# Splitting the kept weights on GpSimd and dividing the mix on ScalarE in a fused attention and feed-forward kernel

## The chip, the cores and the metric

One core of a Trainium2 chip runs the whole kernel. The metric is the device time of one execution in microseconds (us). The engines are TensorE (PE in the profile), its weight loader (PEld), VectorE (DVE), ScalarE (ACT), GpSimd (POOL) and SyncE (SP), which issues the DMAs of weights and output.

## The reference

Eight blocks (the batch) of 128 rows and 512 columns pass through a layer norm, a cross-attention with 32 query heads in 8 groups, a residual add, and a feed-forward stage that looks up a mix of 64 bias rows:

```python
x = x + _L0_xattn_ref(_layernorm(x, axis=-1), ctx_4096, ctx_4096, pos_BxS2, mask_BxSxS2_ik0, Wq, Wk, Wv, Wo)
x = x + _L0_ffn_ref(_layernorm(x, axis=-1), router_weight, router_bias, expert_bias)

def _L0_ffn_ref(hidden_states, router_weight, router_bias, expert_bias):
    logits = jnp.einsum('th,eh->te', flat, router_weight) + router_bias      # 64 logits a row
    scores = jax.nn.softmax(logits, axis=-1)
    topk_w, topk_idx = jax.lax.top_k(scores, K_TOP)                          # K_TOP = 8
    w_sum = topk_w.sum(axis=-1, keepdims=True)
    w_dense = jnp.zeros((T, E), dtype=scores.dtype).at[jnp.arange(T)[:, None], topk_idx].add(topk_w)
    bias_mix = jnp.einsum('te,eh->th', w_dense, expert_bias)
    out = flat * w_sum + bias_mix
```

So a row's output is x + layernorm(x) * w_sum + the mix of the eight kept rows of expert_bias.

## The kernel before

Every engine has its own program, written in the order in which it runs; the engines wait for one another by semaphores that count up. Attention runs over 8 groups (g) and in each over the 8 blocks (b), one block a **step**. In a step TensorE computes the scores of the block two ahead, transposes the probabilities (probT), multiplies block b-1 by Wo into outp, multiplies probabilities and values into attnT, and projects a query seven steps ahead. Numbers are split into a high and a low part (names with _hi and _lo) for the matmuls; ScalarE makes the high part and VectorE or GpSimd the low one.

The feed-forward stage is woven into the 8 steps of the last group (g = 7, `last=True`) and a tail behind them. "Step 4" is below always step 4 of the last group. The stage of a block b is spread over steps:

- step b+1: `ffn_stats(b)` on VectorE (ff_stats, ff_mv, ff_var), then `ffn_rstd(b)` on GpSimd (ff_rstd, ff_mr).
- step b+2: TensorE transposes the block and forms its 64 logits in bank proj[0]; VectorE closes the step with `ffn_max(b)`: ff_shift, ff_logit, ff_negmax. ScalarE, which waits for ff_negmax, then makes ff_exp, and behind it in its order v_hi and pT_hi of the next step.
- step b+3: `ffn_keep(b)` on VectorE: the eight largest (ff_top), ff_rest (the exponentials with those eight set to zero), ff_rsum = 1/sum, ff_kept = ff_exp - ff_rest, and ff_kept split into ff_split. TensorE transposes ff_split (`ffn_kept`, L1185, just before the last head's Wo matmuls of the step), ScalarE copies it to ff_splitT, TensorE multiplies it by the split expert_bias (`ffn_mix`, L1193 and L1194) into bank proj[1], GpSimd makes ff_weight, ff_scale and ff_bias, ScalarE ff_y = x * scale + bias, and VectorE closes the block in `ffn_out`: ff_out = mix * ff_rsum + ff_y. SyncE stores ff_out.

The order on VectorE in step b of the last group is mask_scores, `ffn_keep(b-3)`, lo_p (pT_lo), row_max (negmax), accumulate (resid), `ffn_stats(b-1)`, invert_sums, lo_o (oT_lo), `ffn_max(b-2)`, `ffn_out(b-3)`. Steps 6 and 7 have no scores left, so no mask_scores, row_max or softmax division (GpSimd's `soften`, L412). On ScalarE the order is v_hi, pT_hi, ff_splitT, ff_xT, ff_y, the four exponentials (probs), oT_hi, ff_exp. TensorE's instructions are in one row too: where the transposition of ff_split waits, the Wo matmuls, the probability times value matmuls and the logits stand behind it. Blocks 5 to 7 of the feed-forward stage end in the tail.

Of the kernel before, what the change touches and what calls it, by code (L numbers as in the profile page):

```python
# [19 lines left out]
F32 = mybir.dt.float32  # L20
# [3 lines left out]
ALU = mybir.AluOpType  # L24
ACT = mybir.ActivationFunctionType
# [3 lines left out]
B, S, E = 8, 128, 512  # L29
# [38 lines left out]
FF = 2  # L68
# [3 lines left out]
def xattn_ffn(nc, x, ctx, pos, mask, rope, wq, wk, wv, wo, router, router_bias, expert_bias, out):  # L72
    with ExitStack() as stack:
# [3 lines left out]
        def at(name, cols, dt, offset, parts=P):  # L77
            return nc.alloc_sbuf_tensor_at(name, [parts] + cols, dt, offset=base + int(offset * kib))
# [4 lines left out]
        def sem(name):  # L83
            return stack.enter_context(nc.semaphore(name))
# [15 lines left out]
        ff_y = at("ff_y", [FF, E], F32, 58)  # L100
# [3 lines left out]
        ff_out = at("ff_out", [2, E], F32, 68)  # L104
        ff_logit = at("ff_logit", [NX], F32, 72)
        ff_exp = at("ff_exp", [FF, NX], F32, 72.25)
        ff_rest = at("ff_rest", [FF, NX], F32, 72.75)
        ff_kept = at("ff_kept", [NX], F32, 73.25)
# [53 lines left out]
        ff_top = at("ff_top", [TOP], F32, 206.65625)  # L162
        ff_kept_sum = at("ff_kept_sum", [1], F32, 206.6875)
        ff_rsum = at("ff_rsum", [FF], F32, 75.25)
        ff_weight = at("ff_weight", [1], F32, 75.28125)
        ff_scale = at("ff_scale", [2], F32, 75.3125)
        ff_bias = at("ff_bias", [2], F32, 75.34375)
# [88 lines left out]
        f_rsum = sem("f_rsum")  # L256
# [10 lines left out]
        f_keptT = sem("f_keptT")  # L267
        f_keptTs = sem("f_keptTs")
        f_mix = sem("f_mix")
        f_out = sem("f_out")  # L270

        def projection_bank(u):
# [90 lines left out]
        def _(pool):  # L363
# [46 lines left out]
            def soften(p, count):  # L410
                pool.wait_ge(rsum_done, count)
                pool.tensor_tensor(probs[:, p], probs[:, p], rsum[:, p, :].unsqueeze(2).broadcast_to([P, GH, S]),  # L412
                                   ALU.mult).then_inc(soft_done, 1)
# [18 lines left out]
            def step(g, b, first=False, last=False):  # L432
                n = b + g * B
                if not (first and b < 2):
                    lo_v(g, b, first)
                if not (first and b == 0) and not (last and b + AHEAD - 1 >= B):
                    rotate((KV * NH + AHEAD - 1 + b, g, B), (b + AHEAD - 1) // GH % NH)
                if b < GH and not last:
                    lo_a(wq_lo[:, b], wq_hi[:, b], b % RA, A_Q + GH + b + 1 + g * GH)
                if b == 0 and not first:  # L440
                    for h in range(GH):
                        lo_b(wo_lo[:, h, :], wo_hi[:, h, :], h, KB * C + h + 1 + g * GH)
                if last and b == 0:
                    pool.wait_ge(f_ebhi, 1)
                    pool.tensor_tensor(ff_eb_lo[:, :], ebias[:, :], ff_eb_hi[:, :].bitcast(F32), ALU.subtract).then_inc(f_eblo, 1)
                if last:
                    ffn(b)
                if first and b == 0:
                    lo_v(0, 1, True)
                if not (last and b + FIRST >= B):  # L450
                    soften(b % 2, n + FIRST + 1)

            def ffn(b):
                if b >= 3:
                    ffn_weight(b - 3)
                if 1 <= b < B + 1:
                    ffn_rstd(b - 1)

            def ffn_rstd(b):

                pool.wait_ge(f_var, b + 1)
                if b >= 2:
                    pool.wait_ge(f_bias, b - 1)
                pool.tensor_tensor(ff_rstd[:, b % 2:b % 2 + 1], ff_var[:, :], power[:, 0:1], ALU.pow).then_inc(f_rstd, 1)
                pool.wait_ge(f_rstd, b + 1)
                pool.tensor_tensor(ff_mr[:, b % 2:b % 2 + 1], ff_mv[:, 0:1], ff_rstd[:, b % 2:b % 2 + 1], ALU.mult).then_inc(f_mr, 1)

            def ffn_weight(b):

# [19 lines left out]
                    step(g, b)  # L489
            for b in range(B):  # L490
                step(KV - 1, b, last=True)
            for b in range(B, B + 3):
                ffn(b)


# [1 line left out]
        def _(act):  # L497
# [146 lines left out]
            def ffn(b, part):  # L644
                if part == 0 and b >= 3:
                    ffn_kept(b - 3)
                if part == 0 and b >= 2:
                    ffn_xT(b - 2)
                if part == 0 and b >= 3:
                    ffn_scale(b - 3)  # L650
                if part == 1 and b >= 2:
                    ffn_exp(b - 2)

            def ffn_xT(b):
                act.wait_ge(f_xT, b + 1)
                if b >= 1:
                    act.wait_ge(f_raw, b)
                act.activation(ff_xT[:, :], logit_bank[b][:, :], ACT.Copy).then_inc(f_xTs, 1)

            def ffn_scale(b):  # L660

                act.wait_ge(f_scale, b + 1)
                act.wait_ge(f_bias, b + 1)
                if b >= FF:
                    act.wait_ge(f_out, b - FF + 1)
                act.activation(ff_y[:, b % FF, :], resid[:, b, :], ACT.Identity,
                               bias=ff_bias[:, b % 2:b % 2 + 1], scale=ff_scale[:, b % 2:b % 2 + 1]).then_inc(f_y, 1)

            def ffn_exp(b):
                act.wait_ge(f_max, b + 1)  # L670
# [20 lines left out]
            ffn_kept(B - 3)  # L691
            ffn_exp(B - 2)
            ffn_scale(B - 3)
            ffn_xT(B - 1)
            ffn_kept(B - 2)
            ffn_exp(B - 1)
# [6 lines left out]
        def _(dve):  # L703
# [183 lines left out]
            def ffn(b, part):  # L887
                if part == 0 and b >= 3:
                    ffn_keep(b - 3)
                if part == 1 and b >= 1:  # L890
                    ffn_stats(b - 1)
                if part == 2 and b >= 2:
                    ffn_max(b - 2)
                if part == 2 and b >= 3:
                    ffn_out(b - 3)

            def ffn_stats(b):

# [29 lines left out]
            def ffn_keep(b):  # L928

                exp, rest = ff_exp[:, b % FF, :], ff_rest[:, b % FF, :]  # L930
                dve.wait_ge(f_exp, b + 1)
                dve.max(ff_top[:, :], exp).then_inc(f_top, 1)
                dve.wait_ge(f_top, b + 1)

                dve.match_replace(rest, ff_top[:, :], exp, 0.0).then_inc(f_rest, 1)
                if b >= 2:
                    dve.wait_ge(f_out, b - 1)
                dve.reciprocal(ff_rsum[:, b % FF:b % FF + 1], ff_sum[:, b % FF:b % FF + 1]).then_inc(f_rsum, 1)
                dve.wait_ge(f_rest, b + 1)
                dve.tensor_tensor(ff_kept[:, :], exp, rest, ALU.subtract).then_inc(f_kept, 1)  # L940
                if b >= 1:
                    dve.wait_ge(f_weight, b)
                dve.tensor_reduce(ff_kept_sum[:, :], ff_top[:, :], X_AXIS, ALU.add).then_inc(f_ksum, 1)
                dve.wait_ge(f_kept, b + 1)
                if b >= 1:
                    dve.wait_ge(f_keptT, b)
                dve.tensor_copy(ff_split[:, 0, :], ff_kept[:, :]).then_inc(f_khi, 1)
                dve.wait_ge(f_khi, b + 1)
                dve.tensor_tensor(ff_split[:, 1, :], ff_kept[:, :], ff_split[:, 0, :].bitcast(F32), ALU.subtract).then_inc(f_klo, 1)

            def ffn_out(b):

                dve.wait_ge(f_y, b + 1)
                if b >= 2:
                    dve.wait_ge(dma_out[b % 2], 16 * (b // 2))
                dve.wait_ge(f_mix, b + 1)
                dve.scalar_tensor_tensor(ff_out[:, b % 2, :], mixes[b][:, :], ff_rsum[:, b % FF:b % FF + 1], ff_y[:, b % FF, :],
                                         ALU.mult, ALU.add).then_inc(f_out, 1)
# [11 lines left out]
            ffn_stats(B - 1)  # L970
            ffn_keep(B - 2)
            ffn_max(B - 1)
            ffn_out(B - 3)
            ffn_keep(B - 1)
            ffn_out(B - 2)
            ffn_out(B - 1)
# [3 lines left out]
        def _(pe):  # L980
# [152 lines left out]
            def ffn(b, part):  # L1133
                if part == 0 and b >= 2:
                    ffn_xT(b - 2)
                if part == 0 and b >= 3:
                    ffn_kept(b - 3)
                if part == 1 and b >= 2:
                    ffn_logits(b - 2)
                if part == 1 and b >= 3:  # L1140
                    ffn_mix(b - 3)
# [32 lines left out]
            def ffn_kept(b):  # L1174

                pe.wait_ge(f_klo, b + 1)
                if b == 0:
                    pe.wait_ge(f_colsums, 1)
                elif b < B - 2:
                    pe.wait_ge(f_out, b)  # L1180
                elif b == B - 2:
                    pe.wait_ge(exp_done, STEPS)
                else:
                    pe.wait_ge(ot_lo, STEPS)
                pe.transpose(mixes[b][:, 0:S], ff_split[:, :, :].rearrange("p a k -> p (a k)").bitcast(F32), ident[:, :]).then_inc(f_keptT, 1)  # L1185
# [79 lines left out]
```

## Time and profile before

| | us |
|---|---|
| median of 3 runs (lowest to highest) | 622.12 (621.84 to 622.55) |
| the profiled execution, own time | 622.68 |
| its span in the trace | 620.8 |
| TensorE busy, of the span | 603.8 |
| VectorE busy | 421.0 |
| ScalarE busy | 347.2 |
| GpSimd busy | 323.1 |

The profiled execution lies 0.56 us above the median; the span is shorter than its own time by 1.9 us of start and end. TensorE is busy for almost the whole span, but the stage around the change is the last 50 us, and whether TensorE waits there is read from that stretch alone.

### The profile page before, as it was taken

The numbers are of one execution on the slowest core, as the hardware profiler recorded it, in microseconds if no ns is written. First come the engines' busy times: TensorE is split into PE (matmuls) and PEld (weight loads), VectorE is DVE, ScalarE is ACT, GpSimd is POOL, SyncE is SP. The second block draws the span as 40 slices with busy tenths as digits, with TensorE's granted clock in tenths as the row PEclk, the third lists the DMA queues.
The fourth block names the chain that finished last, engine by engine and source line by source line (L and its number), as shares of the span: only waits on it lengthen the run. The fifth ranks groups of instructions, "written<-read, shape, count | busy, mean of one in ns | idle before, by whom it ended". The sixth has DMA issues, their size and how long they took to land.

```text
span 620.8 us, 10479 instructions
## 1 busy us (share of the span) xinstructions
PE 603.8 (97%) x3076; PEld 505.9 (81%) x3076; DVE 421.0 (68%) x730; ACT 347.2 (56%) x1008; POOL 323.1 (52%) x342
## 2 busy tenths in 40 slices
PE   8999999899999999999999999999999999999986
PEld 7787888688888888888888888888888888888774
DVE  5565667677667766776677667666766776667886
ACT  5222556476557556655665565557555755575553
POOL 5340778665338533853484347435743664374331
PEclk9999999899999999999999999999999999999997
DMA  8710132201003100310021003000300120000001
GB/s 293 276 59 11 35 119 51 69 21 50 0 1 103 34 1 1 101 34 0 0 101 34 0 0 117 18 0 11 108 17 0 32 70 0 0 2 2 34 35 68
DMA packets 16025, 29.58 MB, mean 48 GB/s; under 512 B 2048, under 2 KB 2176, under 8 KB 16000
## 3 DMA queue, kind: packets, MB, share of 16 engines
q1 hardware_dynamic: 15472, 28.22, 14.6%
q0 software_dynamic: 384, 1.05, 0.5%
q8 instruction: 12, 0.20, 0.1%
q14 instruction: 13, 0.11, 0.1%
q10 hardware_dynamic: 144, 0.00, 0.0%
HBM read 27.17 MB, written 2.10 MB: 47 GB/s over the span
## 4 chain that ended last, share of the span: by engine, by line
PE 85%; POOL 4%; DVE 4%; issue 2%; ACT 2%; DMA 1%; SPq 0%; DVEq 0%; POOLq 0%; ACTq 0%
PE proj L983 11%; PE proj L985 10%; PE proj L984 10%; PE outp L1129 9%; PE outp L1131 9%; PE outp L1130 8%; PE score L1084 8%; PE probT L1097 4%; PE attnT L983 2%; PE outp L985 2%; PE outp L983 2%; PE attnT L985 2%; PE outp L984 2%; PE attnT L984 2%; POOL rot L368 2%
## 5 line engine op out<-in xcount | busy, mean ns | idle before, releaser
L574 ACT ACTIVATE probs<-score,negmax 128x128 f32<-128x128 f32 x256 | 90.3, 366 | 61.2 <-DVE negmax L811 61.2
L368 POOL TENSOR_TENSOR rot<-rot,sinT 128x512 f32<-128x512 f32 x80 | 106.9, 1336 | 30.6 <-ACT rot L506 30.6
L505 ACT ACTIVATE rot<-proj 64x512 f32<-64x512 f32 x72 | 42.7, 594 | 126.7 <-PE proj L985 126.7
L803 DVE SCALAR_TENSOR_TENSOR score<-score,mask_bias 128x512 f32<-128x512 f32 x64 | 44.7, 698 | 97.3 <-PE score L1084 97.3
L412 POOL TENSOR_TENSOR probs<-probs,rsum 128x512 f32<-128x512 f32 x64 | 66.6, 1040 | 83.1 <-DVE rsum L817 83.1
L1129 PE MATMUL outp<-wo_hi,oT_hi 128*128 128x512 f32 x256 | 107.2, 419 | 2.6 <-DVE oT_lo L846 2.3
L983 PE MATMUL proj<-xT_hi,wq_hi 128*128 128x512 f32 x256 | 100.9, 394 | 0.0
L1131 PE MATMUL outp<-wo_hi,oT_lo 128*128 128x512 f32 x256 | 100.7, 394 | 0.0
L985 PE MATMUL proj<-xT_hi,wq_lo 128*128 128x512 f32 x256 | 100.2, 391 | 0.0
L984 PE MATMUL proj<-xT_lo,wq_hi 128*128 128x512 f32 x256 | 100.1, 391 | 0.0
L1130 PE MATMUL outp<-wo_lo,oT_hi 128*128 128x512 f32 x256 | 100.0, 391 | 0.0
L712 DVE TENSOR_TENSOR qT<-qT,rot 128x512 f32<-128x512 f32 x64 | 76.9, 1202 | 27.8 <-POOL rot L368 27.7
L420 POOL TENSOR_TENSOR v_lo<-values,v_hi 128x128 fp32r<-128x128 f32 x64 | 29.5, 462 | 124.9 <-ACT v_hi L581 124.9
L1084 PEld LDWEIGHTS score<-kT,qT 128*128 128x128 f32 x512 | 66.8, 191 | 8.2 <-issue 2.7
L1084 PE MATMUL score<-kT,qT 128*128 (+1 forms) x512 | 67.9, 276 | 2.5 <-DVE qT L712 2.3
L1129 PEld LDWEIGHTS outp<-wo_hi,oT_hi 128*128 128x128 f32 x256 | 48.4, 189 | 12.2 <-DVE oT_lo L846 4.5
L1131 PEld LDWEIGHTS outp<-wo_hi,oT_lo 128*128 128x128 f32 x256 | 48.0, 188 | 11.4
L983 PEld LDWEIGHTS proj<-xT_hi,wq_hi 128*128 128x128 f32 x256 | 48.5, 189 | 10.7 <-issue 0.6
L985 PEld LDWEIGHTS proj<-xT_hi,wq_lo 128*128 128x128 f32 x256 | 48.3, 189 | 10.3
L984 PEld LDWEIGHTS proj<-xT_lo,wq_hi 128*128 128x128 f32 x256 | 48.5, 189 | 9.9
L1130 PEld LDWEIGHTS outp<-wo_lo,oT_hi 128*128 128x128 f32 x256 | 48.4, 189 | 8.2
L574 ACT ACTIVATION_READ_ACCUMULATOR probs<-score,negmax 128x1 f32 x256 | 52.1, 204 | 0.0
(181 smaller groups left out, 1146.6 us busy)
## 6 DMA issues: line engine op xcount, KB each, us to landing
ring_a<-in_wq SPq DMA_DIRECT2D x32, 256.0 KB, 2.6
ring_b<-in_wo SPq DMA_DIRECT2D x32, 256.0 KB, 2.5
ctx_in<-in_ctx SPq DMA_DIRECT2D x8, 256.0 KB, 4.2
ring_b<-in_wv SPq DMA_DIRECT2D x8, 256.0 KB, 7.6
resid<-in_x SPq DMA_DIRECT2D x2, 1024.0 KB, 12.0
ring_a<-in_wk SPq DMA_DIRECT2D x8, 256.0 KB, 2.6
out<-ff_out SPq DMA_DIRECT2D x8, 256.0 KB, 2.0
mask_in<-in_mask SPq DMA_DIRECT2D x1, 512.0 KB, 11.9
```

The source lines that it names most:

```text
L368: pool.tensor_tensor(rot[:, k0 % 2, :], rot[:, k0 % 2, :], sinT[:, half * W:(half + 1) * W], ALU.mult).then_inc(sin_done, 1)
L412: pool.tensor_tensor(probs[:, p], probs[:, p], rsum[:, p, :].unsqueeze(2).broadcast_to([P, GH, S]), ALU.mult).then_inc(soft_done, 1)
L574: last = act.activation(probs[:, p, h, :], heads(score[p][:, :])[:, h, :], ACT.Exp, bias=negmax[:, p, h:h + 1], accum_out=sums[:, p, h:h + 1])
L712: dve.tensor_tensor(dst, dst, rot[:, k % 2, :], ALU.add).then_inc(rope_done, 1)
L803: dve.scalar_tensor_tensor(heads(score[p][:, :]), heads(score[p][:, :]), SCALE, mask_bias[:, b, :].unsqueeze(1).broadcast_to([P, GH, S]), ...
L983: pe.matmul(ps, s_hi, m_hi, start=start, stop=False)
L984: pe.matmul(ps, s_hi, m_lo, start=False, stop=False)
L985: return pe.matmul(ps, s_lo, m_hi, start=False, stop=stop)
L1084: last = pe.matmul(score[p][:, h * S:(h + 1) * S], qT[:, half % 2, h, b % HB * S:(b % HB + 1) * S], kT[:, b0 // B + g, b * S:(b + 1) * S], ...
L1129: pe.matmul(outp[b % 2][:, :], oT_hi[:, cols], w[0], start=h == 0, stop=False)
L1130: pe.matmul(outp[b % 2][:, :], oT_hi[:, cols], w[1], start=False, stop=False)
L1131: pe.matmul(outp[b % 2][:, :], oT_lo[:, cols], w[0], start=False, stop=h == GH - 1).then_inc(o_done, 1)
```

## The change

For the first six blocks three pieces move. The subtraction that gives ff_kept and its split into two halves go from VectorE's `ffn_keep` to a new `ffn_keep` on GpSimd, ahead of `ffn_weight`. VectorE's fused multiply and add becomes two operations: ScalarE copies the mix out of PSUM scaled by ff_rsum (new tile ff_mix, new semaphore f_mixed, new `ffn_mixed`, behind oT_hi and ahead of ff_exp), and GpSimd adds ff_mix and ff_y (new `ffn_out`, behind `soften`). The last two blocks keep their operations on VectorE. TensorE's transposition of ff_split now waits for f_mixed of the block before, where it waited for f_out; SyncE's code is unchanged, its stores wait for f_out as before.

```diff
@@ gpsimd
                 if not (last and b + FIRST >= B):
                     soften(b % 2, n + FIRST + 1)
+                if last and b >= 3:
+                    ffn_out(b - 3)

             def ffn(b):
+                if 3 <= b < B + 1:
+                    ffn_keep(b - 3)
                 if b >= 3:
                     ffn_weight(b - 3)
...
+            def ffn_keep(b):
+
+                pool.wait_ge(f_rest, b + 1)
+                if b >= 1:
+                    pool.wait_ge(f_klo, b)
+                pool.tensor_tensor(ff_kept[:, :], ff_exp[:, b % FF, :], ff_rest[:, b % FF, :], ALU.subtract).then_inc(f_kept, 1)
+                pool.wait_ge(f_kept, b + 1)
+                if b >= 1:
+                    pool.wait_ge(f_keptT, b)
+                pool.tensor_copy(ff_split[:, 0, :], ff_kept[:, :]).then_inc(f_khi, 1)
+                pool.wait_ge(f_khi, b + 1)
+                pool.tensor_tensor(ff_split[:, 1, :], ff_kept[:, :], ff_split[:, 0, :].bitcast(F32), ALU.subtract).then_inc(f_klo, 1)
+
+            def ffn_out(b):
+
+                pool.wait_ge(f_mixed, b + 1)
+                pool.wait_ge(f_y, b + 1)
+                if b >= 2:
+                    pool.wait_ge(dma_out[b % 2], 16 * (b // 2))
+                pool.tensor_tensor(ff_out[:, b % 2, :], ff_mix[:, b % FF, :], ff_y[:, b % FF, :], ALU.add).then_inc(f_out, 1)
...
-            for b in range(B, B + 3):
+            ffn(B)
+            ffn_out(B - 3)
+            for b in range(B + 1, B + 3):
                 ffn(b)
@@ scalar
+                if part == 1 and b >= 3:
+                    ffn_mixed(b - 3)
                 if part == 1 and b >= 2:
                     ffn_exp(b - 2)
...
+            def ffn_mixed(b):
+
+                act.wait_ge(f_mix, b + 1)
+                act.wait_ge(f_rsum, b + 1)
+                if b >= FF:
+                    act.wait_ge(f_out, b - FF + 1)
+                act.activation(ff_mix[:, b % FF, :], mixes[b][:, :], ACT.Copy, scale=ff_rsum[:, b % FF:b % FF + 1]).then_inc(f_mixed, 1)
...
             ffn_scale(B - 3)
+            ffn_mixed(B - 3)
             ffn_xT(B - 1)
@@ vector
-                if part == 2 and b >= 3:
-                    ffn_out(b - 3)
...
-                dve.wait_ge(f_rest, b + 1)
-                dve.tensor_tensor(ff_kept[:, :], exp, rest, ALU.subtract).then_inc(f_kept, 1)
                 if b >= 1:
                     dve.wait_ge(f_weight, b)
                 dve.tensor_reduce(ff_kept_sum[:, :], ff_top[:, :], X_AXIS, ALU.add).then_inc(f_ksum, 1)
+                if b < B - 2:
+                    return
+                dve.wait_ge(f_rest, b + 1)
+                dve.wait_ge(f_klo, b)
+                dve.tensor_tensor(ff_kept[:, :], exp, rest, ALU.subtract).then_inc(f_kept, 1)
...
             ffn_max(B - 1)
-            ffn_out(B - 3)
             ffn_keep(B - 1)
@@ tensor
                 elif b < B - 2:
-                    pe.wait_ge(f_out, b)
+                    pe.wait_ge(f_mixed, b)
```

The first place is VectorE in step 4, from the ff_negmax that closes the step before to pT_lo. Before:

```order
L926 TENSOR_REDUCE ff_negmax<-ff_logit 128x1
L957 SCALAR_TENSOR_TENSOR ff_out<-proj,ff_rsum,ff_y 128x512
L803 SCALAR_TENSOR_TENSOR score<-score,mask_bias 128x512
L932 MAX ff_top<-ff_exp 128x8
L935 MATCH_REPLACE ff_rest<-ff_top,ff_exp 128x64
L938 RECIPROCAL ff_rsum<-ff_sum 128x1
L940 TENSOR_TENSOR ff_kept<-ff_exp,ff_rest 128x64
L943 TENSOR_REDUCE ff_kept_sum<-ff_top 128x1
L947 CAST ff_split<-ff_kept 128x64
L949 TENSOR_TENSOR ff_split<-ff_kept,ff_split 128x64
L840 TENSOR_TENSOR pT_lo<-probT,pT_hi 128x512
```

And now:

```order
L964 TENSOR_REDUCE ff_negmax<-ff_logit 128x1
L843 SCALAR_TENSOR_TENSOR score<-score,mask_bias 128x512
L970 MAX ff_top<-ff_exp 128x8
L975 MATCH_REPLACE ff_rest<-ff_top,ff_exp 128x64
L978 RECIPROCAL ff_rsum<-ff_sum 128x1
L981 TENSOR_REDUCE ff_kept_sum<-ff_top 128x1
L880 TENSOR_TENSOR pT_lo<-probT,pT_hi 128x512
```

Four instructions have left VectorE: ff_out between ff_negmax and the mask, and the three that end in ff_split.

The second place is GpSimd in step 4 (block 1 of the feed-forward stage), from the low part of the values to the last instruction of the step. Before:

```order
L420 TENSOR_TENSOR v_lo<-values,v_hi 128x128
L474 TENSOR_TENSOR ff_weight<-ff_kept_sum,ff_rsum 128x1
L480 TENSOR_SCALAR ff_scale<-ff_weight,ff_rstd 128x1
L482 TENSOR_SCALAR ff_bias<-ff_weight,ff_mr 128x1
L464 TENSOR_TENSOR ff_rstd<-ff_var,power 128x1
L466 TENSOR_TENSOR ff_mr<-ff_mv,ff_rstd 128x1
L412 TENSOR_TENSOR probs<-probs,rsum 128x512
```

And now:

```order
L422 TENSOR_TENSOR v_lo<-values,v_hi 128x128
L479 TENSOR_TENSOR ff_kept<-ff_exp,ff_rest 128x64
L483 CAST ff_split<-ff_kept 128x64
L485 TENSOR_TENSOR ff_split<-ff_kept,ff_split 128x64
L501 TENSOR_TENSOR ff_weight<-ff_kept_sum,ff_rsum 128x1
L507 TENSOR_SCALAR ff_scale<-ff_weight,ff_rstd 128x1
L509 TENSOR_SCALAR ff_bias<-ff_weight,ff_mr 128x1
L470 TENSOR_TENSOR ff_rstd<-ff_var,power 128x1
L472 TENSOR_TENSOR ff_mr<-ff_mv,ff_rstd 128x1
L414 TENSOR_TENSOR probs<-probs,rsum 128x512
L493 TENSOR_TENSOR ff_out<-ff_mix,ff_y 128x512
```

The three small instructions stand behind v_lo and ahead of ff_weight; the add is last, behind the softmax division.

The third place is GpSimd in the tail, from the rstd of block 7. Before:

```order
L464 TENSOR_TENSOR ff_rstd<-ff_var,power 128x1
L466 TENSOR_TENSOR ff_mr<-ff_mv,ff_rstd 128x1
L474 TENSOR_TENSOR ff_weight<-ff_kept_sum,ff_rsum 128x1
L480 TENSOR_SCALAR ff_scale<-ff_weight,ff_rstd 128x1
L482 TENSOR_SCALAR ff_bias<-ff_weight,ff_mr 128x1
```

And now:

```order
L470 TENSOR_TENSOR ff_rstd<-ff_var,power 128x1
L472 TENSOR_TENSOR ff_mr<-ff_mv,ff_rstd 128x1
L493 TENSOR_TENSOR ff_out<-ff_mix,ff_y 128x512
L501 TENSOR_TENSOR ff_weight<-ff_kept_sum,ff_rsum 128x1
L507 TENSOR_SCALAR ff_scale<-ff_weight,ff_rstd 128x1
L509 TENSOR_SCALAR ff_bias<-ff_weight,ff_mr 128x1
```

The add of block 5 now stands between ff_mr of block 7 and the weights of block 6.

## Rows read from the trace of the kernel before

**Rows 1.** The page: busy time of each engine, and the chain that ended last.

```profile
PE 603.8 (97%) x3076; PEld 505.9 (81%) x3076; DVE 421.0 (68%) x730; ACT 347.2 (56%) x1008; POOL 323.1 (52%) x342
PE 85%; POOL 4%; DVE 4%; issue 2%; ACT 2%; DMA 1%; SPq 0%; DVEq 0%; POOLq 0%; ACTq 0%
```

**Rows 2.** Timeline, VectorE, steps 3 to 6: start, us, what, idle before.

```profile
569.92 0.22 DVE L926 TENSOR_REDUCE ff_negmax<-ff_logit 128x1 f32<-128x64 f32 x1
...
571.00 0.21 DVE L935 MATCH_REPLACE8 ff_rest<-ff_top,ff_exp 128x64 f32<-128x64 f32 x1
...
577.22 0.22 DVE L926 TENSOR_REDUCE ff_negmax<-ff_logit 128x1 f32<-128x64 f32 x1
577.36 0.74 DVE L957 SCALAR_TENSOR_TENSOR ff_out<-proj,ff_rsum,ff_y 128x512 f32<-128x512 f32 x1
578.02 0.69 DVE L803 SCALAR_TENSOR_TENSOR score<-score,mask_bias 128x512 f32<-128x512 f32 x1
578.62 0.21 DVE L932 MAX8 ff_top<-ff_exp 128x8 f32<-128x64 f32 x1
...
579.68 0.22 DVE L949 TENSOR_TENSOR ff_split<-ff_kept,ff_split 128x64 fp32r<-128x64 f32 x1
...
584.31 0.51 DVE L916 SCALAR_TENSOR_TENSOR ff_shift<-ff_colsum,ff_mr,rbias 128x64 f32<-128x64 f32 x1
...
585.17 0.22 DVE L926 TENSOR_REDUCE ff_negmax<-ff_logit 128x1 f32<-128x64 f32 x1
...
593.12 0.22 DVE L926 TENSOR_REDUCE ff_negmax<-ff_logit 128x1 f32<-128x64 f32 x1
...
599.32 0.22 DVE L926 TENSOR_REDUCE ff_negmax<-ff_logit 128x1 f32<-128x64 f32 x1
```

**Rows 3.** Timeline, TensorE: the transposition of ff_split, and one mix.

```profile
572.07 0.27 PE L1185 MATMUL proj<-ident,ff_split 128*128 128x128 f32 x1
...
579.96 0.33 PE L1185 MATMUL proj<-ident,ff_split 128*128 128x128 f32 x1 [0.67 <-DVE ff_split L949]
...
595.26 0.33 PE L1185 MATMUL proj<-ident,ff_split 128*128 128x128 f32 x1
...
597.95 0.40 PE L1194 MATMUL proj<-ff_eb_lo,ff_splitT 128*128 128x512 f32 x1
```

**Rows 4.** Timeline, GpSimd, steps 3 and 4.

```profile
570.90 0.46 POOL L420 TENSOR_TENSOR v_lo<-values,v_hi 128x128 fp32r<-128x128 f32 x1 [0.29 <-ACT v_hi L581]
...
583.70 1.04 POOL L412 TENSOR_TENSOR probs<-probs,rsum 128x512 f32<-128x512 f32 x1
```

**Rows 5.** Timeline, ScalarE, end of steps 3 and 4.

```profile
577.48 0.35 ACT L674 ACTIVATE ff_exp<-ff_logit,ff_negmax 128x64 f32<-128x64 f32 x1 [1.75 <-DVE ff_negmax L926]
...
583.05 0.62 ACT L635 ACTIVATE oT_hi<-attnT 128x512 fp32r<-128x512 f32 x1
```

**Rows 6.** Timeline, GpSimd, first group: instructions back to back.

```profile
106.45 1.30 POOL L377 TENSOR_TENSOR wo_lo<-ring_b,wo_hi 128x512 fp32r<-128x512 f32 x1
107.71 1.73 POOL L368 TENSOR_TENSOR rot<-rot,sinT 128x512 f32<-128x512 f32 x1
```

**Rows 7.** Timeline, VectorE, the same place.

```profile
106.53 1.77 DVE L712 TENSOR_TENSOR qT<-qT,rot 128x512 f32<-128x512 f32 x1 [0.59 <-POOL rot L368]
```

**Rows 8.** Timeline, GpSimd, the tail.

```profile
612.03 0.19 POOL L466 TENSOR_TENSOR ff_mr<-ff_mv,ff_rstd 128x1 f32<-128x1 f32 x1
612.19 0.19 POOL L474 TENSOR_TENSOR ff_weight<-ff_kept_sum,ff_rsum 128x1 f32<-128x1 f32 x1
612.48 0.30 POOL L480 TENSOR_SCALAR ff_scale<-ff_weight,ff_rstd 128x1 f32<-128x1 f32 x1
```

**Rows 9.** Timeline, VectorE, the tail.

```profile
612.31 0.23 DVE L949 TENSOR_TENSOR ff_split<-ff_kept,ff_split 128x64 fp32r<-128x64 f32 x1
...
612.90 0.28 DVE L923 SCALAR_TENSOR_TENSOR ff_logit<-probT,ff_rstd,ff_shift 128x64 f32<-128x64 f32 x1 [0.17 <-DVE ff_shift L916]
...
614.01 0.22 DVE L932 MAX8 ff_top<-ff_exp 128x8 f32<-128x64 f32 x1
```

More of the change, by code:

```diff
@@ L164, in xattn_ffn @@
         ff_rsum = at("ff_rsum", [FF], F32, 75.25)
+        ff_mix = at("ff_mix", [FF, E], F32, 76)
         ff_weight = at("ff_weight", [1], F32, 75.28125)
@@ L269, in xattn_ffn @@
         f_mix = sem("f_mix")
+        f_mixed = sem("f_mixed")
         f_out = sem("f_out")
@@ L933, in ffn_keep @@
                 dve.wait_ge(f_top, b + 1)
+                if b >= 2:
+                    dve.wait_ge(f_kept, b - 1)
                 dve.match_replace(rest, ff_top[:, :], exp, 0.0).then_inc(f_rest, 1)
@@ L953, in ffn_out @@
                 dve.wait_ge(f_y, b + 1)
-                if b >= 2:
-                    dve.wait_ge(dma_out[b % 2], 16 * (b // 2))
+                dve.wait_ge(f_out, b)
+                dve.wait_ge(dma_out[b % 2], 16 * (b // 2))
                 dve.wait_ge(f_mix, b + 1)
```

## The prediction

> **What bounds the kernel now.** I read the page first, then the timeline of the last 50 us engine by engine. TensorE is busy for 97% of the span and holds 85% of the chain that ended last [rows 1], but those are averages, and the change touches only steps 3 to 7 of the last group and the tail. There I measure each step between two starts of ff_negmax, called N: 569.92, 577.22, 585.17, 593.12, 599.32 [rows 2]. So step 3 lasts 7.30, steps 4 and 5 7.95 each, step 6 6.20, and step 7 repeats step 6. In step 4 TensorE stands idle 0.67 before it transposes ff_split, waiting for VectorE [rows 3], so the step is a loop: ff_negmax, ff_out, mask, ff_top to ff_split on VectorE; then from TensorE's transposition at 579.96 over ScalarE's copies, y and exponentials and VectorE's oT_lo and ff_shift to the next N at 585.17, which is 5.21 [rows 2, 3]. In step 6 that second part is 599.32 - 595.26 = 4.06 (no scores, it runs over the Wo matmuls and the residual add). VectorE's freed time therefore counts only where it makes the transposition start earlier. Everything turns on one figure: how long after N TensorE can transpose ff_split. Now it is 2.15 in step 3 (572.07), 2.74 in steps 4 and 5 (579.96), 2.14 in step 6 (595.26).
>
> **The steps, part by part.** *ff_out leaves VectorE*: its slot is 578.02 - 577.36 = 0.66 [rows 2]. But ff_top needs ff_exp, which ScalarE starts 0.26 after N. Step 3 has no ff_out yet and shows what is left then: ff_rest starts at 571.00, N + 1.08, and ends at N + 1.29. With ff_out, ff_top started at N + 1.40 in step 4 [rows 2]. In steps 6 and 7 there is no mask, ff_out only fills the wait for ff_exp, and its leaving is worth nothing.
>
> *The split on GpSimd*: it needs ff_rest (N + 1.29) and stands behind v_lo, which starts at N + 0.98 (570.90) and lasts 0.46 [rows 4]; instructions there overlap by 0.04 (106.45 + 1.30 against 107.71) [rows 6]. So it starts at N + 1.40. No row shows these three on GpSimd. v_lo, 128 elements, is 0.46, ff_weight, one element, 0.19 [rows 4, 8]; a line through both gives 0.32 for 64 elements with two inputs, and I take 0.26 for the one-input cast. Dependent instructions lie 0.10 apart (ff_weight ends 612.38, ff_scale starts 612.48) [rows 8]. The chain is x = 0.32 + 0.10 + 0.26 + 0.10 + 0.32 = 1.10. TensorE followed ff_split's end by 0.06 (579.68 + 0.22 against 579.96) [rows 2, 3]. The transposition now starts at N + 1.40 + x + 0.06 = N + 2.56. Bounds of x: 0.75 if each takes ff_weight's 0.19 (with 0.18 of gaps), 1.56 if each takes v_lo's 0.46. The value between is nearest in size to both.
>
> The Trainium skill, GPSIMD Engine Reference, section 4.1 Engine selection, speaks against this move: it puts elementwise adds and subtractions on VectorE, GpSimd being about twice as slow with two inputs. Doubling 0.22, 0.20 and 0.22 makes x about 1.46, an estimate from that page, and a total near 626.0.
>
> Against the present steps this gives
> - step 3: 2.56 + 5.21 = 7.77, +0.47
> - steps 4 and 5: 7.77 against 7.95, -0.18 each
> - step 6: 2.56 against 2.14, +0.42
> - step 7: the same +0.42, and 0.1 more: the mix of block 3 ends 3.09 behind the transposition (598.35 against 595.26) [rows 3], ScalarE's scaled copy takes 0.7 (oT_hi is 0.62 [rows 5], a scale pointer more), GpSimd's add 1.30, which ends at about N + 1.1 and holds v_lo up.
>
> Sum: +1.05; as a function of x, 5x - 4.46.
>
> *Costs taken as nothing.* ff_mixed on ScalarE: in steps 3 to 5 it starts at oT_hi's end (583.67), ends near 584.4, and ff_exp waits for ff_negmax until 0.26 after N with 1.75 idle [rows 5]; in steps 6 and 7 half a microsecond of the cover is left. Without it the 0.7 would fall on ff_exp and on each step. The add on GpSimd in steps 3 to 5 follows the division, which ends 584.74 = N - 0.43 [rows 4], ends near N + 0.95, just ahead of v_lo at N + 0.98: hidden with nothing to spare. ff_weight, ff_scale, ff_bias move behind the split: bias ends near N + 3.3, ff_y can't start before the transposition + 1.02 = N + 3.58. TensorE's wait on f_mixed is met a step early; the stores of SyncE end a step ahead of use.
>
> **A lock between VectorE and GpSimd.** ff_shift, two SBUF inputs of 64 elements, takes 0.51 in step 4 (its logit twin, with one input in PSUM, 0.28 [rows 9]); it ends at 584.82, 0.08 after GpSimd's division of the probabilities ends at 584.74 [rows 2, 4]. qT <- qT,rot likewise took 1.77, held until 0.55 after wo_lo's end. It was then served ahead of GpSimd's next instruction, which stretched to 1.73 [rows 6, 7]. So in steps 3 to 5 ff_shift should again get through between the division and the add. ff_rest, with one tensor input, kept 0.21 under v_lo [rows 2, 4]; I let the other one-input instructions pass freely.
>
> In the tail it costs. GpSimd's order is now ff_mr of block 7, the add of block 5, then the weights [rows 8]. The add's inputs are there, so it starts at 612.19, when VectorE has the split of block 6 (612.31) and ff_shift of block 7 still to do [rows 9], both with two SBUF inputs. The add lasts 1.30, to 613.49; the split ends 0.08 later, 613.57; from its end to ff_logit it was 0.36 (612.54 to 612.90) [rows 9], so ff_logit starts at 613.93, +1.03. ff_out of block 5 leaves VectorE there, worth 0.05 at most (ff_top at 614.01 then waits for ff_exp); the cast of blocks 6 and 7 directly follows ff_kept, 0.1 more. Tail: +1.08. All behind it shifts along: the last transposition, mix and store. The tail up to the last Wo matmuls is TensorE's own and takes the split of block 5 with some 0.5 to spare. The tail's bounds are +0.1 (VectorE gets in first) and +1.4.
>
> The Trainium skill, SBUF — State Buffer, section SBUF: two separate sides, calls this an exclusive lock held for a whole instruction by whichever started first. By it the add would hold both VectorE instructions out until it ends; this trace agrees, with the 0.51 above. Who goes first when both wait it doesn't say.
>
> **Sum.** +1.05 + 1.08 = +2.13. On the profiled execution's own 622.68 that is 624.8; the median of the runs is 0.56 lower, so I predict 624.3.
>
> **The rivals.**
> - *No stall in the tail* (12%): the add of block 5 starts after 612.7 instead of 612.2, so VectorE's two instructions go first. Then +1.05 + 0.1: 623.3. Against it: GpSimd followed ff_mr with the next instruction after 0.16 [rows 8].
> - *Short instructions* (6%): x = 0.75. Steps -0.7, tail +1.08: 622.5.
> - *Long instructions* (8%): x = 1.56, as v_lo: steps +3.34, tail +1.08: 626.5.
> - *The lock goes the other way* (6%): the add follows the division before the waiting ff_shift, 1.3 more in each of steps 3 to 5: 628.2. Rows 6 and 7 speak against it.
> - *Faster* (6%): VectorE is the pacer of steps 4 and 5 and is relieved of 1.17 in each. If x were 0.48 (three of 0.10 and the small gaps) the transposition would come at N + 1.94, each of the two steps 0.80 shorter; step 3 and 6 gain nothing, because TensorE gets there at N + 2.15 by itself. With no stall in the tail: -1.5, 620.6. It decides at x below 0.63 and no stall; GpSimd's shortest here, 0.19 for one element, is against it.
>
> **How the numbers follow.** The forecast has 62%, its own range is 623.4 to 625.2. Low 622.6 to high 626.6 takes in the first and third rival and leaves out 18%. A measurement of this kernel tells 0.2% (1.24 us, 623.36) from no change: slower holds 0.62 + 0.08 + 0.06 = 0.76, within it 0.12 + 0.06 = 0.18, faster 0.06.
>
> **What would show it.** In the profile after: the transposition of ff_split at N + 2.5 to 2.6 in every step with GpSimd as releaser, instead of 2.15, 2.74 and 2.14; steps of about 7.8 where they were 7.30 and 7.95, and 6.6 where they were 6.2; GpSimd's three small ones at 0.32, 0.26, 0.32; ff_mix 0.7 with ff_exp still waiting behind; in the tail a split or ff_shift on VectorE stretched to more than 1 us, ending 0.1 behind GpSimd's add. Wrong it would be if x is far from 1.10 (five steps count it), if ff_shift in steps 3 to 5 is longer than 0.5, or if the tail's add lies elsewhere.

## The result and the profile after

Over 20 executions each, the changed kernel takes 623.07 us (622.01 to 626.60) and the kernel before 621.89 (620.55 to 623.32). The ratio is 1.0028 with a 95% interval of 1.0016 to 1.0040: slower by 1.7 us, between 1.0 and 2.5. The ratio is that of the means, 623.38 and 621.64; the medians differ by 1.18. The prediction was slower, by 2.1, with a median of 624.3.

The two profiled executions have the same span, 620.8, although the kernels differ. One profiled execution lost some 1.5 us, and the other did not, in a stretch that the change does not touch. The next rows are windows of the kernel before, 109 to 125 us: length, busy time and count of PE, PEld, DVE, ACT, POOL, then the granted clock, DMA share, GB/s.

```profile
109.00:118.00 9.00, 6.73 (x32) 5.13 (x31) 7.07 (x6) 4.82 (x8) 9.00 (x7) 1.00 0.36 95
118.00:125.00 7.00, 7.00 (x31) 5.87 (x30) 2.86 (x5) 2.69 (x10) 2.23 (x3) 0.76 0.10 27
```

The same windows of the changed kernel:

```profile
109.00:118.00 9.00, 6.75 (x31) 5.07 (x31) 7.07 (x6) 4.82 (x8) 9.00 (x7) 1.00 0.34 90
118.00:125.00 7.00, 7.00 (x40) 6.02 (x40) 3.34 (x6) 2.84 (x11) 2.60 (x3) 1.00 0.10 33
```

Before, TensorE, which had been busy 6.73 of 9 us, is granted 0.76 of its clock over the next 7 us and gets through 31 matmuls; after, at full clock, through 40. The first ff_negmax of the feed-forward stage then starts at 569.92 in the kernel before and at 568.41 in the changed one. So spans of single executions can't be compared here. I compare the **stage**: from the first ff_negmax (block 0, the end of step 2) to the start of the last ff_out. Before it is 617.55 - 569.92 = 47.63. This is the timeline of the changed kernel, VectorE (start, us, what, idle before):

```profile
568.41 0.22 DVE L964 TENSOR_REDUCE ff_negmax<-ff_logit 128x1 f32<-128x64 f32 x1
...
576.11 0.22 DVE L964 TENSOR_REDUCE ff_negmax<-ff_logit 128x1 f32<-128x64 f32 x1
...
577.18 0.21 DVE L975 MATCH_REPLACE8 ff_rest<-ff_top,ff_exp 128x64 f32<-128x64 f32 x1
...
582.94 0.51 DVE L954 SCALAR_TENSOR_TENSOR ff_shift<-ff_colsum,ff_mr,rbias 128x64 f32<-128x64 f32 x1
...
583.80 0.22 DVE L964 TENSOR_REDUCE ff_negmax<-ff_logit 128x1 f32<-128x64 f32 x1
...
591.49 0.22 DVE L964 TENSOR_REDUCE ff_negmax<-ff_logit 128x1 f32<-128x64 f32 x1
592.22 0.23 DVE L970 MAX8 ff_top<-ff_exp 128x8 f32<-128x64 f32 x1 [0.51 <-ACT ff_exp L713]
...
598.01 0.22 DVE L964 TENSOR_REDUCE ff_negmax<-ff_logit 128x1 f32<-128x64 f32 x1
...
604.63 0.22 DVE L964 TENSOR_REDUCE ff_negmax<-ff_logit 128x1 f32<-128x64 f32 x1
...
611.42 1.22 DVE L992 TENSOR_TENSOR ff_split<-ff_kept,ff_split 128x64 fp32r<-128x64 f32 x1
612.56 0.27 DVE L954 SCALAR_TENSOR_TENSOR ff_shift<-ff_colsum,ff_mr,rbias 128x64 f32<-128x64 f32 x1
612.87 0.28 DVE L961 SCALAR_TENSOR_TENSOR ff_logit<-probT,ff_rstd,ff_shift 128x64 f32<-128x64 f32 x1
...
617.47 0.75 DVE L1000 SCALAR_TENSOR_TENSOR ff_out<-attnT,ff_rsum,ff_y 128x512 f32<-128x512 f32 x1 [1.55 <-PE attnT L1236]
```

The stage is 617.47 - 568.41 = 49.06, 1.43 longer, inside the interval of the measured difference. The steps are 7.70, 7.69, 7.69, 6.52 and 6.62, where [rows 2] gave 7.30, 7.95, 7.95, 6.20 and for step 7 the same again (6.19). In the tail, VectorE's split of block 6 (611.42) lasts 1.22, where it was 0.23 [rows 9].

TensorE's timeline of the changed kernel, the transpositions of ff_split in steps 3, 4, 6 and 7, answers to [rows 3]:

```profile
570.89 0.33 PE L1227 MATMUL proj<-ident,ff_split 128*128 128x128 f32 x1 [0.17 <-POOL ff_split L485]
...
578.58 0.33 PE L1227 MATMUL proj<-ident,ff_split 128*128 128x128 f32 x1 [0.42 <-POOL ff_split L485]
...
593.96 0.33 PE L1227 MATMUL proj<-ident,ff_split 128*128 128x128 f32 x1 [0.42 <-POOL ff_split L485]
...
600.58 0.33 PE L1227 MATMUL proj<-ident,ff_split 128*128 128x128 f32 x1 [0.29 <-POOL ff_split L485]
```

TensorE now waits for GpSimd each time, and starts 2.48, 2.47, 2.47 and 2.57 behind ff_negmax. GpSimd's timeline of the same kernel shows why, and the tail:

```profile
577.09 0.46 POOL L422 TENSOR_TENSOR v_lo<-values,v_hi 128x128 fp32r<-128x128 f32 x1 [0.15 <-ACT v_hi L610]
577.51 0.32 POOL L479 TENSOR_TENSOR ff_kept<-ff_exp,ff_rest 128x64 f32<-128x64 f32 x1
577.89 0.24 POOL L483 CAST ff_split<-ff_kept 128x64 fp32r<-128x64 f32 x1
578.21 0.32 POOL L485 TENSOR_TENSOR ff_split<-ff_kept,ff_split 128x64 fp32r<-128x64 f32 x1
...
582.33 1.04 POOL L414 TENSOR_TENSOR probs<-probs,rsum 128x512 f32<-128x512 f32 x1
583.32 1.30 POOL L493 TENSOR_TENSOR ff_out<-ff_mix,ff_y 128x512 f32<-128x512 f32 x1
...
599.08 0.46 POOL L422 TENSOR_TENSOR v_lo<-values,v_hi 128x128 fp32r<-128x128 f32 x1
...
611.15 0.19 POOL L472 TENSOR_TENSOR ff_mr<-ff_mv,ff_rstd 128x1 f32<-128x1 f32 x1
611.29 1.26 POOL L493 TENSOR_TENSOR ff_out<-ff_mix,ff_y 128x512 f32<-128x512 f32 x1
612.52 0.19 POOL L501 TENSOR_TENSOR ff_weight<-ff_kept_sum,ff_rsum 128x1 f32<-128x1 f32 x1
```

The split starts when v_lo is through, at N + 1.40 (N is the start of ff_negmax, as in the prediction), and takes 578.53 - 577.51 = 1.02. The add in the tail starts right behind ff_mr and ends at 612.55; VectorE's split ends at 612.64, 0.09 later.

### The profile page after: what moved, and what is told of

It reads as the page before. It is cut to its first block, busy times and chain, and to the rows that moved or that the text cites. A ratio compares the mean times of both kernels' runs of the same rounds, so it can differ in the third digit from the quotient of the medians.

```text
span 620.8 us, 10506 instructions
## 1 busy us (share of the span) xinstructions
PE 602.7 (97%) x3076; PEld 505.2 (81%) x3076; DVE 415.6 (67%) x706; ACT 350.9 (57%) x1014; POOL 335.9 (54%) x366
## 4 chain that ended last, share of the span: by engine, by line
PE 83%; POOL 7%; DVE 4%; issue 2%; ACT 1%; DMA 1%; SPq 1%; POOLq 0%; DVEq 0%; ACTq 0%
PE proj L1025 10%; PE proj L1027 10%; PE proj L1026 10%; PE outp L1171 9%; PE outp L1173 9%; PE outp L1172 8%; PE score L1126 8%; PE probT L1139 4%; PE attnT L1025 2%; PE outp L1027 2%; PE outp L1025 2%; PE outp L1026 2%; PE attnT L1027 2%; PE attnT L1026 2%; POOL rot L370 2%
```

## The experiments

The theory to test has three parts. (a) Each step is as long as TensorE's transposition of ff_split is late behind ff_negmax, unless TensorE gets there itself at 2.1. (b) Moving ff_out gives something back in steps 4 and 5 alone. (c) The tail is longer because a GpSimd instruction that reads SBUF shuts out VectorE's instructions with two SBUF inputs. The stage of each profiled execution, by the same rows as above:

| kernel | step 3 | 4 | 5 | 6 | 7 | tail | stage | ratio to before (95%) |
|---|---|---|---|---|---|---|---|---|
| before | 7.30 | 7.95 | 7.95 | 6.20 | 6.19 | 12.04 | 47.63 | |
| changed | 7.70 | 7.69 | 7.69 | 6.52 | 6.62 | 12.84 | 49.06 | 1.0028 (1.0016 to 1.0040) |
| split only | 7.70 | 8.30 | 8.31 | 6.54 | 6.55 | 12.04 | 49.44 | 1.0042 (1.0027 to 1.0057) |
| out only | 7.31 | 7.30 | 7.29 | 6.13 | 6.21 | 12.85 | 47.09 | 0.9994 (0.9982 to 1.0005) |
| changed, tail's order | 7.71 | 7.69 | 7.69 | 6.53 | 6.65 | 12.02 | 48.29 | 1.0003 (0.9993 to 1.0014) |
| out only, tail's order | 7.32 | 7.30 | 7.31 | 6.13 | 6.21 | 12.08 | 46.35 | 0.9985 (0.9973 to 0.9997) |
| the same, copy late | 7.31 | 7.30 | 7.30 | 6.12 | 6.22 | 11.98 | 46.23 | 0.9980 (0.9969 to 0.9992) |
| changed, cast twice | 7.99 | 7.99 | 8.01 | 6.83 | 6.93 | 12.85 | 50.60 | one execution |
| before, add in the tail | 7.31 | 7.95 | 7.96 | 6.19 | 6.20 | 12.92 | 48.53 | one execution |
| before, memset in the tail | 7.31 | 7.95 | 7.95 | 6.18 | 6.20 | 11.91 | 47.50 | one execution |

The columns are differences of neighbouring ff_negmax; the tail runs from the last of them in the steps (block 5) to the last ff_out. Unchanged steps repeat to 0.03 from kernel to kernel, so differences of 0.1 can be read there. The tail is less steady, because the granted clock of TensorE differs in its last microseconds (see the memset below); differences under 0.15 in it aren't read as effects of an edit.

**The split alone.** The changed kernel with ff_out back on VectorE:

```diff
                 if part == 2 and b >= 2:
                     ffn_max(b - 2)
+                if part == 2 and b >= 3:
+                    ffn_out(b - 3)
...
-                if last and b >= 3:
-                    ffn_out(b - 3)
```

(the first pair is VectorE's and the second GpSimd's; GpSimd's add in the tail and ffn_mixed on ScalarE are gone too, and TensorE waits for f_out again).

> Only the split is on GpSimd, ff_out stays on VectorE for all blocks. Counted from the ff_negmax of block 0 to the start of the last ff_out (47.63 us before, 49.06 after). Theory (how long after ff_negmax TensorE can transpose ff_split sets each step): with ff_out back on VectorE ff_rest ends at 1.95, so the transposition comes 3.1 behind ff_negmax in steps 4 and 5, which last 8.3 (7.95 before, 7.69 after); step 3 stays 7.70, steps 6 and 7 6.52; no stall in the tail, which is at 12.15 from the last ff_negmax of the steps (12.04 before). Sum 49.5, 1.9 over before: slower than before by 0.3%. Rival (moving ff_out gave nothing back): steps 4 and 5 stay 7.7 and the sum is 48.2 or less.

The theory holds: 8.30 and 8.31 in steps 4 and 5, stage 49.44. GpSimd's timeline of this kernel in step 4:

```profile
578.55 0.46 POOL L422 TENSOR_TENSOR v_lo<-values,v_hi 128x128 fp32r<-128x128 f32 x1 [1.41 <-ACT v_hi L606]
579.59 0.32 POOL L477 TENSOR_TENSOR ff_kept<-ff_exp,ff_rest 128x64 f32<-128x64 f32 x1 [0.58 <-DVE ff_rest L970]
```

With ff_out on VectorE the split waits for ff_rest (0.58 idle), no longer for v_lo, and the transposition comes 3.08 behind ff_negmax. Only the tail is the one of before.

**The output alone.** The changed kernel with `ffn_keep` whole on VectorE:

```diff
             def ffn(b):
-                if 3 <= b < B + 1:
-                    ffn_keep(b - 3)
                 if b >= 3:
                     ffn_weight(b - 3)
...
```

(behind the cut, VectorE's `ffn_keep` gets its three instructions back for all blocks).

> Only ff_out is moved (scaled copy on ScalarE, add on GpSimd, tail as in the changed kernel); the split stays on VectorE. Theory: the transposition comes at 2.15 in steps 4 and 5, where TensorE itself arrives, so they last 7.35 (7.95 before); steps 3, 6, 7 stay at 7.30, 6.2, 6.2 because ff_top waits for ff_exp; the tail keeps the whole stall, 12.85 against 12.04. Sum 47.2 against 47.63 before: 0.4 less. Rival (GpSimd's add holds back v_lo or VectorE's two-input instructions in the steps): steps 4 and 5 stay near 7.9 and the sum is 48.4.

The transposition comes at N + 2.08 and steps 4 and 5 last 7.30, 0.65 less than before, so the add costs nothing there. This is TensorE's timeline of step 4:

```profile
578.38 0.60 PE L1199 MATMUL proj<-ident,resid 128*128 128x128 f32 x4
579.01 0.33 PE L1220 MATMUL proj<-ident,ff_split 128*128 128x128 f32 x1
```

The transpositions of the residual end at 578.98 and that of ff_split starts at 579.01: nothing is left to gain by an earlier split. Steps 6 and 7 hardly change (-0.07, +0.02). The tail has the whole +0.8, against 1.35 gained in the steps: stage 47.09, ratio not clear of 1. Together with the run before, part (b) is shown.

**The order in the tail.** The changed kernel, and then the one with the output alone, with GpSimd's last add behind the small instructions of block 6:

```diff
             ffn(B)
-            ffn_out(B - 3)
-            for b in range(B + 1, B + 3):
-                ffn(b)
+            ffn(B + 1)
+            ffn_out(B - 3)
+            ffn(B + 2)
```

> The changed kernel with GpSimd's add of block 5 behind the three small instructions of block 6 instead of ahead of them. Theory (VectorE's split of block 6 and ff_shift of block 7 were locked out by the add): the split is back to 0.23 us, the tail is 12.1 instead of 12.84, sum 48.3. Rival (the tail is longer because ff_top waits for ff_exp and TensorE for VectorE anyway, or the stall only moves to the next two-input instruction): tail 12.7 or more.

> Both: only ff_out is moved, and the tail's add stands behind the small instructions of block 6. Theory: steps 4 and 5 at 7.35, the others as before, tail 12.05: sum 46.4, 1.2 less than before, ratio to before 0.998. Rival of the second run: steps as before and sum 47.6, no change.

The tail goes from 12.84 to 12.02 and from 12.85 to 12.08. VectorE's timeline in the tail of the changed kernel with this order:

```profile
611.33 0.23 DVE L992 TENSOR_TENSOR ff_split<-ff_kept,ff_split 128x64 fp32r<-128x64 f32 x1
611.47 0.28 DVE L954 SCALAR_TENSOR_TENSOR ff_shift<-ff_colsum,ff_mr,rbias 128x64 f32<-128x64 f32 x1
612.01 0.28 DVE L961 SCALAR_TENSOR_TENSOR ff_logit<-probT,ff_rstd,ff_shift 128x64 f32<-128x64 f32 x1 [0.26 <-PE probT L1213]
...
613.65 0.21 DVE L986 TENSOR_TENSOR ff_kept<-ff_exp,ff_rest 128x64 f32<-128x64 f32 x1
```

The split is back to 0.23. The add now runs from 612.00 to 613.28, while VectorE has ff_logit (one input in PSUM), ff_negmax and ff_top to do, and is over before ff_kept, the next instruction with two SBUF inputs. In place of the stall ff_logit waits 0.26 for TensorE's logits. These are TensorE's logits of block 7 in the kernel before and in this one:

```profile
611.59 1.10 PE L1171 MATMUL probT<-routerT,ff_xT 128*128 128x64 f32 x8 [0.69 <-ACT ff_xT L658]
```

```profile
610.70 1.10 PE L1213 MATMUL probT<-routerT,ff_xT 128*128 128x64 f32 x8 [0.78 <-ACT ff_xT L689]
```

ff_logit starts 1.31 behind their start in both (612.90 and 612.01). So it waited for the logits in the kernel before too: the 0.17 of idle time that [rows 9] shows before it, with ff_shift named as the releaser, was that wait. In the changed kernel ff_logit starts 2.07 behind them (610.80 and 612.87), held by VectorE's own stall. With the other order the wait for the logits is 0.09 longer than before. The candidate is the copy on ScalarE, which stands ahead of ff_xT of block 7.

**The copy behind ff_xT.** The last kernel with ScalarE's two instructions in the tail swapped:

```diff
             ffn_scale(B - 3)
-            ffn_mixed(B - 3)
             ffn_xT(B - 1)
+            ffn_mixed(B - 3)
```

> The fourth run's kernel (only ff_out moved, the tail's add behind the small instructions of block 6) with ScalarE's scaled copy of block 5 behind ff_xT of block 7 instead of ahead of it. Theory: ff_xT of block 7 follows TensorE's transposition again at once, ff_logit of block 7 comes 7.39 behind the last ff_negmax of the steps instead of 7.48, sum 46.25 against 46.35, ratio to before 0.998. Rival (ff_shift, not the logits, holds ff_logit in the tail): 7.48 stays.

ff_logit of block 7 comes 7.38 behind the ff_negmax of block 5 instead of 7.48, and the stage is 46.23. This version is faster than the kernel before by 0.2%: medians 620.17 against 621.60 over 12 and 17 executions, ratio 0.9980 (0.9969 to 0.9992). What the swap of the two instructions adds, 0.1 us, is read from the start of ff_logit; the ratios of the last two versions don't tell them apart.

**The cast twice.** The changed kernel with one more cast in the chain, and the next one waiting for it:

```diff
-                pool.tensor_copy(ff_split[:, 0, :], ff_kept[:, :]).then_inc(f_khi, 1)
+                pool.tensor_copy(ff_split[:, 0, :], ff_kept[:, :]).then_inc(f_again, 1)
+                pool.wait_ge(f_again, b + 1)
+                pool.tensor_copy(ff_split[:, 0, :], ff_kept[:, :]).then_inc(f_khi, 1)
```

> The changed kernel with the cast of the high half done twice in a row on GpSimd for each of the first six blocks, the second waiting for the first: the chain of small instructions is 0.31 longer (0.24 and a gap of 0.07). Theory (each of the five steps is as long as the transposition is late): steps 8.0, 8.0, 8.0, 6.8, 6.9 against 7.70, 7.69, 7.69, 6.52, 6.62, the tail as it was (12.84), sum 50.6 against 49.06. Rival (some steps are paced by something else, ScalarE's exponentials or TensorE): fewer than five steps grow, sum below 50.2.

All five steps grow, by 0.29, 0.30, 0.32, 0.31 and 0.31, together 1.53, and the tail by 0.01. Part (a) is shown: the chain of small instructions stands in the way five times over.

**An add and a memset in the tail of the kernel before.**

```diff
-            for b in range(B, B + 3):
+            ffn(B)
+            pool.wait_ge(f_mr, B)
+            pool.wait_ge(f_spare, 1)
+            pool.tensor_tensor(spare[:, 2, :], spare[:, 0, :], spare[:, 1, :], ALU.add)
+            for b in range(B + 1, B + 3):
                 ffn(b)
```

(the two inputs are cleared in step 1 of the last group, which f_spare reports; the other kernel has `pool.memset(spare[:, 2, :], 0.0)` in place of the last two lines before the loop, and clears nothing in step 1).

> The kernel before with one more add of 128x512 on GpSimd (two SBUF inputs, on a spare tile) in the tail, between ff_mr of block 7 and the weight of block 6; its two inputs are cleared in step 1. Nobody waits for it but the weights of block 6. Theory (lock): VectorE's split of block 6 takes some 1.1 to 1.2 instead of 0.23 and ends 0.1 behind the add; the tail is 12.85 against 12.04. Rival (in the changed kernel the tail was longer through the copy on ScalarE or the late weights): the split stays at 0.23 and the tail within 12.2.

> The kernel before with a memset of 128x512 on GpSimd in the same place instead of the add: it writes SBUF and reads nothing. Theory (what holds VectorE out is a GpSimd instruction that reads SBUF): the split of block 6 stays at 0.23, tail 12.05. Rival (any GpSimd instruction of that size shuts out VectorE's two-input instructions): the split and ff_shift are stretched until 0.1 after the memset's end.

VectorE's timeline with the add, which ran on GpSimd from 612.04 to 613.40:

```profile
612.04 0.23 DVE L958 TENSOR_TENSOR ff_split<-ff_kept,ff_split 128x64 fp32r<-128x64 f32 x1
612.19 1.29 DVE L925 SCALAR_TENSOR_TENSOR ff_shift<-ff_colsum,ff_mr,rbias 128x64 f32<-128x64 f32 x1
613.51 0.28 DVE L932 SCALAR_TENSOR_TENSOR ff_logit<-probT,ff_rstd,ff_shift 128x64 f32<-128x64 f32 x1
```

The expectation named the split, and that was a miss: split and add started at the same time and the split got through; ff_shift, the next with two SBUF inputs, was held and ended at 613.48, 0.08 behind the add. The tail is 12.92, where the theory said 12.85, and nothing of the change is in this kernel: the add alone makes the stall. With the memset, GpSimd's timeline and then VectorE's:

```profile
610.46 0.53 POOL L495 MEMSET spare<- 128x512 f32 x1
```

```profile
610.48 0.22 DVE L953 TENSOR_TENSOR ff_split<-ff_kept,ff_split 128x64 fp32r<-128x64 f32 x1
610.63 0.28 DVE L920 SCALAR_TENSOR_TENSOR ff_shift<-ff_colsum,ff_mr,rbias 128x64 f32<-128x64 f32 x1
```

Both lie wholly under the memset and take what they always take. The tail is even 0.13 shorter, but not through the memset. TensorE's last transposition of ff_split, before and with the memset:

```profile
615.35 0.47 PE L1185 MATMUL attnT<-ident,ff_split 128*128 128x128 f32 x1 [0.85 <-DVE ff_split L949]
```

```profile
613.53 0.33 PE L1189 MATMUL attnT<-ident,ff_split 128*128 128x128 f32 x1 [1.34 <-DVE ff_split L953]
```

It is 0.14 shorter with the memset. In the microsecond ahead of it the granted clock was 0.50 (the lower level, 1.2 GHz) in the kernel before and 1.00 (2.4 GHz) with the memset. Part (c) is shown as far as the two instructions reach: an add that reads SBUF holds VectorE's two-input instruction until it ends, and a memset that only writes SBUF doesn't. A GpSimd instruction with one SBUF input was not tried. The Trainium skill agrees: SBUF — State Buffer, section SBUF: two separate sides, which limits the lock of a two-input VectorE instruction to GpSimd instructions that read SBUF.

## Why the prediction was right

Direction, mechanism and place were right; the sum was too large by 0.7 (2.13 against 1.43 in the stage). The number alone would not have shown that. The median, 623.07, lies inside low to high but below the forecast's own range of 623.4 to 625.2, and next to the 623.3 of the rival without a stall in the tail. It is the trace that decides between them: the stall is there (1.22 instead of 0.23). The base was also high: the three runs of the kernel before that gave 622.12 are all among its slower eleven of twenty, and the median of the twenty is 621.89. By its own terms the prediction did this:

| term | predicted | measured |
|---|---|---|
| x, the three small instructions | 1.10 | 1.02 |
| transposition behind ff_negmax | 2.56 | 2.47 |
| step 3 | +0.47 | +0.40 |
| steps 4 and 5 | -0.18 each | -0.26 each |
| step 6 | +0.42 | +0.32 |
| step 7 | +0.52 | +0.43 |
| tail | +1.08 | +0.80 |

- *x and what multiplies it.* The lengths were right (0.32, 0.24, 0.32 against 0.32, 0.26, 0.32); the gap between dependent instructions is 0.06 to 0.08 and not the 0.10 read between ff_weight and ff_scale. Together with 0.05 instead of 0.06 to TensorE this is 0.09 a step, and five steps make 0.4 of the 0.7. The twice-cast run shows that the factor five is right. The estimate of 1.46 doubled all three lengths, the one-input cast too; doubling the two subtractions alone gives 1.26. Neither came: at 64 elements the subtractions take 0.32 against VectorE's 0.22, and the cast 0.24 against 0.20.
- *ff_out leaves VectorE.* Worth 0.65 in steps 4 and 5 and nothing in 6 and 7, as said: in step 6 ff_top waits 0.51 for ff_exp, and with the output alone these steps move by -0.07 and +0.02. That it is spent by the later split is shown by the two single runs: -0.65 with the output alone, +0.35 with the split alone, -0.26 with both.
- *Step 7's extra 0.1.* v_lo starts at 599.08, N + 1.07 instead of N + 0.97 in step 6; the transposition there is 0.10 later.
- *Costs taken as nothing.* The scaled copy is 0.70 on average and ff_exp still waits for ff_negmax behind it, 1.17 in steps 3 to 5 and 0.5 in steps 6 and 7. The add in steps 3 to 5 is 1.30 and ended before v_lo, with 0.15 idle between.
- *Who goes first at the lock.* ff_shift stayed at 0.51 in steps 3 to 5, through between the division and the add. That rival is out.
- *The tail.* The term that was mis-sized: ff_logit came 0.85 later in the tail, not 1.03 (8.24 behind the ff_negmax of block 5 against 612.90 - 605.51 = 7.39), because the prediction carried over the 0.36 from the split's end to ff_logit. Of these, 0.17 were idle time in which ff_logit waited for TensorE's logits, as the run with the other order shows. The stall hides that wait: ff_logit follows ff_shift by 0.04 (612.83 to 612.87), and the split's end by 612.87 - 612.64 = 0.23. The add was 1.26 instead of 1.30. The 0.1 for the later cast did not show either (0.25 from ff_kept to the cast in block 7, 0.26 before), while the 0.05 for ff_out may have: from ff_logit to the last ff_out it is 4.60 after and 4.65 before.

The rival of no stall in the tail is what the run with the other order shows on purpose: ratio 1.0003, no change that the runs can tell, with 0.66 more in the stage. The faster rival needed a split as early as TensorE gets there; the runs with the output alone reach that by not moving the split. They also show that the rival was priced too high: it gave steps 4 and 5 0.80 each with a transposition at N + 1.94, but in those runs TensorE arrives at N + 2.08 and no earlier, and 0.65 is all that was there. Measured alone, the split costs 1.81 of the stage and the output gains 0.54, or 1.28 with the other order in the tail.

## What to carry to other kernels

A short chain between two engines is priced by where it ends, not by the busy time it takes off an engine: three instructions of 0.2 us moved alone from VectorE to GpSimd ended some 0.35 to 0.4 later in each of five steps, and TensorE waited for them each time. Moving work off the engine that paces a loop pays only up to the point where the next one arrives by itself (here 2.1 us behind ff_negmax) and only in the steps where that engine is not waiting anyway. Place a large GpSimd instruction that reads SBUF where VectorE's next instructions are not of the kind with two SBUF inputs (here ff_logit, with an operand in PSUM, ff_negmax and ff_top kept their lengths beside it); three small instructions earlier it cost 0.8 us here.

## What was not expected of the hardware

- The ten profiled executions fall into two groups by one stretch that no edit touches. In all of them TensorE was busy 6.71 to 6.75 of the 9 us from 109 to 118. From 118 to 125 the granted clock was 1.00 in four, and the first ff_negmax of the stage started at 568.1 to 568.4. It was 0.76 to 0.81 in the other six, and that ff_negmax started at 569.6 to 569.9. Of 20 executions of the kernel before, nine lie between 620.55 and 621.17 and eleven between 621.84 and 623.32, which fits, but no kernel was profiled in both groups. What decides it was not tried.
- Where VectorE's two-input instruction and GpSimd's add start in the same hundredth of a microsecond (both 612.04), VectorE's went first and the add took 1.36 instead of 1.26 to 1.30.
